# A new order for the first two blocks of an attention and mixture-of-experts kernel

## What is computed

```python
def reference(x, ctx, ...):
    h = layernorm(x)                                  # no gain, no bias
    q, k, v = h @ Wq.T + bq, ctx @ Wk.T + bk, ctx @ Wv.T + bv
    p = softmax(q_heads @ k_heads.T / sqrt(16))       # 16 heads of 16, 77 keys
    x = x + tanh(g_xattn) * ((p @ v_heads) @ Wo.T + bo)

    h = layernorm(x) * ln_g + ln_b
    top2, idx = top_k(h @ Wr, 2)                      # 7 experts
    gates = softmax(top2)
    # each expert takes the first 732 tokens that choose it, first choices ahead
    routed = sum over both choices: gate * (silu(h @ W1[e]) * (h @ W3[e])) @ W2[e]
    shared = (silu(h @ W1s) * (h @ W3s)) @ W2s
    return x + tanh(g_ffn) * (routed + shared)
```

## Time and profile before

| | |
|---|---|
| median of 3 runs | 910.91 us (910.74 to 912.74) |
| the profiled execution: its own time | 909.93 us |
| its span, first to last instruction | 908.2 us |
| mean granted TensorE clock | 0.968 of full speed |
| PE busy | 826.7 us (91%) |
| DVE busy | 609.4 us (67%) |
| ACT busy | 385.8 us (42%) |
| POOL busy | 326.0 us (36%) |

### The profile page before, as it was taken

How to read it: one execution, slowest core, us unless ns; L and a number is a source line. 1 busy time by engine, 2 the same in 40 slices (tenths; PEclk the granted TensorE clock), 3 DMA queues, 4 the chain that set the end, 5 groups by cost and what they waited for, 6 DMA issues and landing times.

```text
span 908.2 us, 14547 instructions
## 1 busy us (share of the span) xinstructions
PE 826.7 (91%) x5130; PEld 713.9 (79%) x5130; DVE 609.4 (67%) x1360; ACT 385.8 (42%) x718; POOL 326.0 (36%) x259
## 2 busy tenths in 40 slices
PE   4766799998999999999899999999999999999991
PEld 3533686885866858758687789999999999999991
DVE  5566877878779778787777766566665656565340
ACT  3254235336344254263535345354444545453330
POOL 5171403104013031040112840846547281823333
PEclk9868799999999999999999999999999999999996
DMA  6542041122400423203113332334434333431111
GB/s 170 139 140 63 10 117 36 44 74 49 117 15 21 116 49 69 56 27 93 36 43 119 110 99 93 83 87 103 85 102 82 86 74 104 97 66 19 16 19 19
DMA packets 97297, 66.93 MB, mean 74 GB/s; under 512 B 57910, under 2 KB 84716, under 8 KB 97240
## 3 DMA queue, kind: packets, MB, share of 16 engines
q1 hardware_dynamic: 43624, 55.40, 21.8%
q0 software_dynamic: 53088, 10.30, 8.3%
q10 hardware_dynamic: 528, 0.52, 0.2%
HBM read 37.38 MB, written 14.27 MB: 57 GB/s over the span
## 4 chain that ended last, share of the span: by engine, by line
PE 68%; DVE 13%; issue 7%; POOL 2%; ACT 1%; DVEq 0%; DMA 0%; POOLq 0%
PE bank L1367 19%; PE bank L1369 18%; PE bank L1368 18%; PE bank L1583 2%; PE bank L1584 2%; PE bank L1585 2%; DVE hidden L1097 2%; PE bank L1448 1%; PE bank L1621 1%; DVE bn_parts L1049 1%; DVE normed_heads L1101 1%; DVE row_max L1087 1%; DVE float_data L1170 1%; PE bank L1549 1%; DVE float_data L1068 1%
## 5 line engine op out<-in xcount | busy, mean ns | idle before, releaser
L1367 PE MATMUL bank<-split_operands 128*128 128x366 f32 (+4 forms) x1148 | 385.7, 336 | 15.2 <-DVE split_operands L1017 9.7
L1368 PE MATMUL bank<-split_operands 128*128 128x366 f32 (+4 forms) x1148 | 379.4, 331 | 0.0
L1369 PE MATMUL bank<-split_operands 128*128 128x366 f32 (+4 forms) x1148 | 379.3, 330 | 0.0
L1367 PEld LDWEIGHTS bank<-split_operands 128*128 128x128 f32 (+1 forms) x1148 | 217.2, 189 | 36.9 <-DVE split_operands L1022 7.2
L1369 PEld LDWEIGHTS bank<-split_operands 128*128 128x128 f32 (+1 forms) x1148 | 216.5, 189 | 12.4
L1368 PEld LDWEIGHTS bank<-split_operands 128*128 128x128 f32 (+1 forms) x1148 | 217.5, 189 | 9.7
L836 POOL DMA_INDIRECT out<-float_data,scatter_now x42 | 125.5, 2987 | 179.6 <-issue 93.0
L1350 DVE TENSOR_TENSOR hidden<-bank,float_data 128x366 f32<-128x366 f32 x112 | 60.4, 540 | 113.9 <-PE bank L1369 113.9
L1003 ACT ACTIVATE float_data<-bank 128x366 f32<-128x366 f32 x112 | 53.5, 477 | 113.7 <-PE bank L1369 113.7
L1000 ACT CAST split_operands<-hidden 128x366 fp32r<-128x366 f32 x112 | 55.7, 497 | 68.4 <-DVE hidden L1350 67.3
L812 POOL DMA_INDIRECT float_data<-z_scratch,gather_now x42 | 72.1, 1718 | 14.9 <-issue 14.0
(11 more groups left out here) (152 smaller groups left out, 1099.9 us busy)
## 6 DMA issues: line engine op xcount, KB each, us to landing
float_data<-in_L_ffn_W SPq DMA_DIRECT2D x21, 1024.0 KB, 8.6
split_operands<-split_operands SPq DMA_DIRECT2D x96, 128.0 KB, 2.3
float_data<-in_x SPq DMA_DIRECT2D x8, 512.0 KB, 4.8
z_scratch<-float_data SPq DMA_DIRECT2D x8, 512.0 KB, 3.1
out<-float_data SPq DMA_DIRECT2D x7, 512.0 KB, 2.8
split_operands<-split_operands SPq DMA_DIRECT2D x8, 192.0 KB, 3.8
float_data<-in_L_ffn_W1s SPq DMA_DIRECT2D x2, 512.0 KB, 4.1
float_data<-in_L_ffn_W3s SPq DMA_DIRECT2D x2, 512.0 KB, 4.9
```

Of the source, the lines that this page charges most:

```text
L1367: pe.matmul(o, lhs[0], rhs[0], start=first, stop=False)
L1368: pe.matmul(o, lhs[0], rhs[1], start=False, stop=False)
L1369: return pe.matmul(o, lhs[1], rhs[0], start=False, stop=last)
```

## The change

Nothing of the arithmetic changes, and the periods from block 2 on keep their order. What changes is the opening (`first_period`) and the period of block 1.

1. **Loads.** The host lays out ctx, the four attention weights and the small vectors by partition. ctx comes in one DMA instead of two, the value and output weights in one instead of seventeen, seven small inputs (four vectors, two gates, the router) in one instead of seven. SP has 12 load DMAs ahead of its first copy of keys, where 35 stood ahead of the first store of keys.
2. **Order of block 0.** DVE takes the statistics of x before it splits the query weights. The value and output weights are split on POOL instead of DVE. `maxima` of block 0 follow at once on the queries; `project_values` stands behind all four and uses PSUM banks 6 and 7 in pairs. The key copies `kbd` wait for the high halves alone.
3. **Shared weights.** `shared_weights(0)` puts ACT's casts of loads 0 to 2 and POOL's six subtractions ahead of `maxima_T` of block 0, `shared_weights(1)` the casts of loads 3 to 5 between `project` and block 1's `maxima_T`, `shared_rest` the last four subtractions. ACT's exponentials run without casts between them. Loads 4 and 5 have buffers of their own.
4. **Block 1 inside block 0's scores.** `norm(n)` runs ahead of `first_scores(b)`, `transpose_x(n)` between `first_scores` and `scores(b, 0)`, `queries(n)` between `scores(b, 0)` and `scores(b, 1)`. pv writes two banks, 4 and 5, in turn (`pv_bank`) and waits for `pv_read`, the DVE transpose that reads them.
5. **Block 0's norm and routing.** All of block 1's `maxima` stand on DVE ahead of `project_out`, `norm2` of block 0. `transpose_z(0)` lies between the halves of block 1's `scores`. Everything behind it (`logits`, `logits_T`, `choose`, `count`, `counted`, `slots`, `place` of block 0 and the statistics and scaling of block 2's x) moves into the part of the period in which the shared expert of block 0 runs.

The core of the diff:

```diff
 def first_period(do, b):
     n = b.next()
+    do("context")
+    do("weights", 1)
     do("project_keys")
-    do("norm", b)
-    do("keys_lo")
+    do("stats_x", b)
+    do("weights", 0)
+    do("scale_x", b)
+    do("bias_keys")
     do("transpose_x", b)
-    do("norm", n)
+    do("weights", 2)
     do("queries", b)
+    do("queries_out", b)
+    do("keys", b)
+    do("residual", b)
+    do("stack", b)
+    do("shared_weights", 0)
+    for t in range(TT):
+        do("maxima", b, t)
     do("project_values")
-    do("keys", b)
-    do("stack", b)
-    do("maxima", b, 0)
-    do("maxima", b, 1)
-    do("transpose_x", n)
-    do("maxima", b, 2)
-    do("maxima", b, 3)
     do("maxima_T", b)
     do("stack_maxima", b)
+    do("values_out")
+    norm(do, n)
+    do("first_scores", b)
+    do("transpose_x", n)
     do("route_const")
+    do("scores", b, 0)
     do("queries", n)
-    do("first_scores", b)
-    for half in range(2):
-        do("scores", b, half)
+    do("scores", b, 1)
+    do("queries_out", n)
     do("stack", n)
+    do("attention_hi", b)
     do("maxima", n, 0)
     do("maxima", n, 1)
-    do("attention_hi", b)
     do("project", b)
+    do("shared_weights", 1)
     do("maxima", n, 2)
     do("maxima", n, 3)
     do("maxima_T", n)
     do("stack_maxima", n)
+    do("project_out", b)
     do("norm2", b)
-    do("transpose_z", b)
+    do("shared_rest")
     do("first_scores", n)
-    do("logits", b)
-    do("logits_T", b)
-    do("choose", b)
-    do("norm", n.next())
 def period(do, b):
...
     do("scores", b, 0)
     if b.at(1):
-        do("count", f)
-        do("counted", f)
-        do("slots", f)
+        do("transpose_z", f)
     do("scores", b, 1)
+    if b.at(1):
+        nxt("stats_x")
     up(0)
-    do("place", f)
+    if b.at(1):
+        nxt("scale_x")
+        nxt("residual")
+    else:
+        do("place", f)
     do("attention_hi", b)
+    if b.at(1):
+        do("logits", f)
     up(1)
+    if b.at(1):
+        do("logits_T", f)
     nxt("transpose_x")
     up(2)
     do("project", b)
+    do("project_out", b)
     nxt("queries")
+    nxt("queries_out")
     nxt("stack")
     do("norm2", b)
+    if b.at(1):
+        do("choose", f)
     down(0)
     down(1)
     nxt("maxima", 0)
     up(3)
-    do("transpose_z", b)
-    up(4)
+    if b.at(1):
+        do("count", f)
+        do("counted", f)
+        do("slots", f)
+        up(4)
+        do("place", f)
+        do("transpose_z", b)
+    else:
+        do("transpose_z", b)
+        up(4)
     down(2)
     do("logits", b)
...
-            sp.dma_start(sh_stage[h % 3].rearrange("p (k f) -> p k f", k=kk), wsv[m][:, part * kk:(part + 1) * kk])\
+            sp.dma_start(sh_stage[h].rearrange("p (k f) -> p k f", k=kk), wsv[m][:, part * kk:(part + 1) * kk])\
...
+            if h == 5:
+                sp.wait_ge(sig["xT_ready"], 2 * KD)
...
+            if b.at(2):
+                pe.wait_ge(sig["lg_done"], 1)
```

399 lines of the change are left out of this document (218 added, 181 removed).

## The result

The kernel after the change takes **915.12 us** (median of 6 runs, 914.47 to 919.06) beside 911.66 us of the kernel before (6 runs, 910.74 to 912.74): a ratio of **1.0049, interval 1.0036 to 1.0062**. It is slower by 0.5%, some 4.5 us, where the prediction had 910.7 and a range up to 914.8. The profiled execution has a span of 912.8 us against 908.2, so the difference of the spans, 4.6 us, is what has to be found. By their own times (915.07 and 909.93) the two profiled executions differ by 5.1: another 0.5 us lies outside the span, where no row shows its cause.

A forecast was written before the change was run, and what follows sets the result against it. PE was taken as short of work only in the first 100 us, so `up(0)`'s start and work moved behind it count. 12.1 less and 11.9 more made 909.93 into 909.7, the median 910.7 us, range 906.0 to 914.8.

The forecast's parts named there:

- 12.1 earlier: Start of `up(0)`, the first work that fills PE: at 85.5 us instead of 97.56.
- Opening to block 0's first scores: From the first loads to block 0's first scores: these start at 33.9 us, 7.6 earlier than 41.54.
- To block 1's first scores: Block 0's scores and block 1's maxima: block 1's first scores at 69.6 us instead of 77.95.
- First scores to `up(0)`: Block 1's attention, costed by ACT's exponentials, z's transposes and the products: from 69.6 us to `up(0)` at 85.5.
- -3.7 to 0: Unknown cost listed for the low clock in the opening: between 3.7 us less and no change.
- Behind `up(0)`: Work and waits moved behind `up(0)`: 1.5 + 2.0 + 5.0 + 3.4 = 11.9 us late at block 1's logits.
- the wait at `count`: Behind `up(0)`, PE's `count` waits for the maxima that `choose` delays on DVE: +1.6 us, and 0.4 for itself.
- at `place`: Behind `up(0)`, PE's `place` waits for POOL's last entry: +4.1 us, and 0.9 for itself.
- The opening did not keep the high clock: Rival: PE stays at 2.4 GHz through block 1's queries, transposes and maxima; 3.7 us less, 907.0; chance 0.2.
- The shared loads hold ACT: Rival: third shared load lands at 69, delaying ACT's maxima copy; 3.5 more, 914.2; chance 0.28 with other late DMA.
- The routing found no cover: Rival: matmuls behind `count` slip less than thought, so the 11.9 shrink to 9; 907.8 us; chance 0.15.
- The prediction's own sign of being wrong: Wrong if `place` finds its operands ready, or if `up(0)` starts before 83 or after 88 us.

The follow-up runs named there:

- e8: The kernel after the change run once more, unchanged, to see how its runs spread: 917.63 us, 1.0051 of the kernel before.
- e9: Kernel after, with block 0's z transposes ahead of block 1's second pair of scores and POOL's last four subtractions behind z's scaling: 910.94 us, 0.9984 of before.
- e2: Kernel after, with ACT's copy of block 1's transposed maxima ahead of its six shared casts, and POOL's subtractions 6 and 7 later: 917.13 us, 1.0048 of before.
- e3: Kernel after, with block 0's `place` moved from in front of z's transposes to behind block 1's logits: 916.01 us, 1.0042 of before.
- e1: Kernel after, with POOL starting its last four shared-weight subtractions only when DVE has scaled z: 918.80 us, 1.0061 of before.
- e11: Kernel after, with z's transposes and block 0's routing earlier, maxima copy first, counts in another bank, thirteen unread matmuls before block 0's scores: 901.67 us, 0.9878 of before.
- e4: Kernel after, with eleven unread matmuls on TensorE between the transposes of block 1's maxima and block 1's first scores: 914.64 us, 1.0028 of before.

## Why the prediction was wrong, step by step

The structure held (a gain ahead of `up(0)`, a loss behind it), and the sum of 0.2 less became 4.6 more. **The step that failed is the term "12.1 earlier" for `up(0)`**, of which 8.1 came, and in it the way from block 1's first scores to `up(0)`: costed by ACT's exponentials, it was bound by PE at 1.2 GHz.

- *Opening to block 0's first scores*, 7.6 earlier forecast, 5.7 measured. Keys started at 7.26, not 6.6: the key weights landed no earlier. All of the queries ran at the slow pace, where before the last six ran at the fast one, and the maxima started at 22.33, not 20.4. In e8, the same kernel, the first scores stand at 33.41, beside 33.9 forecast: this term is right or wrong by the clock of the execution.
- *To block 1's first scores*, 69.6 forecast, 70.03 measured. The maxima's copy was put at 66.7 and stood at 67.09. What had been lost before came back in block 0's scores, where the window of 36 to 48 has 0.86. In e8 it is the other way round, and there this stage stands at 73.28.
- *First scores to `up(0)`*, 15.9 forecast, 19.4 measured. I costed four pairs of exponentials by ACT, 4.2 us each time, and of the products and scores beside them only one product of 1.9 and the last of 1.0. That holds at the clock of the rows that I took it from. At 1.2 GHz scores (1.99 to 2.10 for two pairs) and products (1.94) stand one behind the other on PE, and 17.13 of the 19.4 us are PE's. Of the clock I had written only a gain, -3.7 to 0, and no loss: that bound was open on the wrong side. e9 shows the price by taking it away (12.2 us). The routing's wait, 5.12 us before, did leave the stretch.
- *Behind `up(0)`*, 11.9 forecast, 12.6 measured: the wait at `count` 1.42 (1.6), at `place` 4.21 (4.1). `place` itself took 1.7 until the transposes began, not 0.9, at the low clock, and from the transposes to the logits it was 5.2, not 5.6. So the two waits held, and that nothing is given back behind the logits held too.
- *The rivals.* The opening did not keep the high clock. Against this rival I had written that only 2 us of waiting lay ahead of `up(0)` when it began low; the row of 95.69 shows 5.12 ahead of the last product. The shared loads hold ACT by 1.7 us (e2), which the forecast contained; the last casts began at 66.04, so the third load had landed by then and not at 69. The routing found no cover, and e3 shows why: DVE is the next bound.
- *The range.* The upper end, 914.8, was set by the shared loads. The low clock in block 1's attention alone was 3.5 us more than the sum, and the second group of runs lies 4 higher again. The prediction's own sign of being wrong, an `up(0)` after 88, was met: it started at 89.43.

e9 comes to the forecast's 910.7 within 0.3 us, and block 1's logits stand at 127.06 against 126.5. But it gets there with an `up(0)` 3.5 us earlier than forecast and 4.1 us more behind it, so this agreement is partly chance.

## What to carry to other kernels

A duration read from a row is one at that row's clock: before a stage of TensorE is costed at nothing beside another engine, it should be summed at 1.2 GHz as well, and the larger of the two engines taken. Work moved from in front of a saturated stretch into it costs its full time and that of the waits it brings (7.5 us here beside the kernel after, 10.9 beside e9), while in front it cost 3.1 at most; there most of it stood beside exponentials. When runs of one kernel fall into groups, a look at the granted clock by stage tells which stretch differs, and a dozen unread matmuls in the gap ahead of it is a cheap test, which here gained some 2 us. A profile stands for the group that its run belongs to, and not for the others.

## What the hardware showed that I had not expected

**DVE and POOL exclude each other in these operations.** The four scalings of z (128x256, one tensor of the buffer in, one out) took 1368 ns each (median by tile) beside POOL's subtractions, of 1285 ns each, and 408 in e1, alone. It is not a slower rate but one of DVE's instructions for each of POOL's. The Trainium skill ("SBUF — State Buffer", SBUF: two separate sides) has the shared port pair of the two engines as an exclusive lock, held for the whole instruction; this trace agrees. Also in e11 one of `choose`'s steps, 0.19 otherwise, took 1.17 where a subtraction of POOL began:

```profile
82.91 0.19 DVE L1279 TENSOR_TENSOR route_tmp<-logits,top_values 128x28 f32<-128x28 f32 x1
83.13 1.17 DVE L1280 TENSOR_TENSOR route_tmp<-route_tmp,expert_minus 128x28 f32<-128x28 f32 x1
```

```profile
82.96 1.29 POOL L792 TENSOR_TENSOR split_operands<-float_data,split_operands 128x512 fp32r<-128x512 f32 x1
```

**A busy TensorE can stay at 1.2 GHz.** In the kernel after it was busy for 17.13 of 19.40 us of block 1's attention, with no wait over 1.9 us, and the granted clock was 0.50 throughout; in e9 the same matmuls in another order had 0.80. What in the order decides it is open: the rows show the waits that went (0.40 and 1.83 us), and in e4's profiled execution work ahead of the stretch did not hold the clock through it.
